# Second cross-attention: scores of all 16 heads on four row tiles of TensorE

## The chip, the cores and the metric

The kernel runs on one core of a Trainium2 chip. The metric is the device time of one execution in microseconds (us). Engines are named as in the profile: PE is TensorE's matmuls and PEld its weight loads, DVE is VectorE, ACT is ScalarE, POOL is GpSimd, SP is SyncE, which here issues the DMAs.

## The reference

The kernel computes two layers on `x` (2 batches, 128 queries, width 128) with a context of 2 x 2048 keys: cross-attention, self-attention, a mixture of experts, and then a second time cross-attention, self-attention and experts. All is float32. The change lies in the second cross-attention:

```python
rq = (iQ @ Wq.T).reshape(b, q, H, ADIM)                    # H = 16 heads of ADIM = 8
kv = (iK @ Wkv.T).reshape(b, s, 2, H, ADIM)                # iK: the context, s = 2048
rk, rv = (kv[:, :, 0], kv[:, :, 1])
scores = jnp.einsum('bqhd,bshd->bhqs', rq, rk) / sqrt(ADIM)
scores = jnp.where(mask[:, None, :, :], jnp.float32(-1e+32), scores)
t = jax.nn.relu(scores + nbias[0]); t = t * t
attn = t / (t.sum(-1, keepdims=True) + IEPS)
o = jnp.einsum('bhqs,bshd->bqhd', attn, rv).reshape(b, q, H * ADIM)
return o @ Wo.T
```

## The kernel before

Each engine has a program written out by hand in one function, and the engines meet on semaphores. An instruction that waits holds up all behind it on its engine.

**Keys and values.** During the first layer's self-attention and experts, gaps of TensorE are filled with the keys and values of the second cross-attention (`fill`, L623 and L628). The keys lie transposed: partition = key dimension (head x 8 + d), column = key. Each key block of 512 columns is copied by ScalarE as float32 and as float32r (`k1_hi`, rounded), and POOL subtracts (L1145) to get the rest, `k1_lo`. Products of float32r operands run in one pass of TensorE; a plain float32 matmul makes two records in the profile.

**The key stack.** The 16 heads are four groups `g` of four heads, 32 key dimensions each. SP then issues 16 DMAs (L441) that copy `k1_hi` and `k1_lo` within SBUF into `kstack`: for each group, the same 32 rows four times, hi, lo, hi, lo, so that one matmul on 128 rows sums hi x hi, lo x hi, hi x lo and lo x lo. The query is made to fit: `q1` is made for each group with its 32 rows repeated four times (four products of `wq1`, L739), ScalarE scales it (L1023), VectorE rounds it and puts the rest in rows 64 to 127 (`q1s`, L1373 and L1374), and `spread_q` (L357) multiplies it with the table `headsel` to give `qbd`: four copies side by side, each with one head's rows and zeros elsewhere. VectorE spreads the first of the eight blocks (batch, group), POOL the others.

**The loop.** A unit `m` is one batch, one group of four heads and two key blocks of 128: 4 heads x 2 blocks x 128 queries = 1024 columns, two PSUM banks. There are 64 units; units m, m+1, m+2 use three slots of two banks in turn. Eight units with the same batch and group follow each other. For each unit
- TensorE: `scores1(m)`, four matmuls of 256 columns (L762), after it waited for the slot's last user, unit m-3;
- VectorE: for seven units of eight one instruction (L1390) that takes the maximum with the negated bias and the minimum with `cap` (mask) and writes `w_ring` (three buffers); ScalarE squares it into `p_ring` (L1057, three buffers);
- for the first unit of eight: ScalarE relu into `w_first` (L1037), POOL multiplies by `keep` (L1156) and squares into `p_first` (L1160). In ScalarE's program this relu stands ahead of the square of the last unit of the eight before;
- TensorE: `weigh_v`, eight matmuls (L783) that weigh the values of nine columns (8 and one of ones) with the probabilities, on four column tiles of 32 columns. Its units run behind: two `scores1`, then two `weigh_v` of units four and more back. Of each eight the first unit (the one through POOL) is weighed last.

When the eight units of a batch and group are weighed, ScalarE copies 128 columns to `oT1` (eight copies). After the loop eight transposes (L800), the division by the sums, the output product and the layer norm follow; self-attention and experts close the kernel.

**Entry.** After the experts of the first layer come the layer norm (VectorE), two transposes, ScalarE's copy `xnT` (L885), the query product, and meanwhile on VectorE a memset of two PSUM banks (L1366) and the making of `keep` (L1368). SP issues the expert weights of the second layer behind the `kstack` DMAs, and some small weights after the last scores.

Of the kernel before, what the change touches and what calls it, by code (L numbers as in the profile page):

```python
# [16 lines left out]
F32 = mybir.dt.float32  # L17
# [7 lines left out]
P = 128  # L25
# [9 lines left out]
QUAD = 4  # L35
NQ = B * H // QUAD
# [57 lines left out]
def build(nc, ins, out):  # L94
    with ExitStack() as ctx:
# [3 lines left out]
        def bc(ap, axis, n):  # L99
# [77 lines left out]
        keep = A.take("keep", (P, B, 2 * S))  # L177
# [39 lines left out]
        cmp1 = A.take("cmp1", (P, 3, B, E1, E1))  # L217
        comb = A.take("comb", (P, B, E1))
# [15 lines left out]
        qbd = A.take("qbd", (P, B, 4, 4, S), F32R)  # L234
# [6 lines left out]
        A = Arena(nc, ctx_at, end)  # L241
# [3 lines left out]
        attn1 = A.take("attn1", (P, B, H, DA))  # L245
        attn1T = A.take("attn1T", (P, T))
# [6 lines left out]
        A2 = Arena(nc, attn0_at, attn0_at + B * H * DH * 4)  # L253
        q1 = A2.take("q1", (P, 4, T))
        q1s = A2.take("q1s", (P, 4, T), F32R)
# [5 lines left out]
        wq1 = A.take("wq1_sb", (P, 4, P))  # L261
# [9 lines left out]
            "w1", "w2", "ctxT2", "mask", "l1w", "kstack", "exp1", "sa")}  # L271
# [32 lines left out]
        q1s_done, qbd_pool = sem("q1s_done"), sem("qbd_pool")  # L304
# [59 lines left out]
        UNITS = NBLK // 2  # L364
        COMBOS = B * 4
        NU = COMBOS * UNITS
        WEIGH_LAG = 3
# [25 lines left out]
        def _(sp):  # L393
# [32 lines left out]
            get(wq1[:], "wq1", "l1w")  # L426
# [34 lines left out]
        def _(pe):  # L461
# [276 lines left out]
            for g in range(4):  # L738
                last = mm(ps[:, g // 2, (g % 2) * T:(g % 2 + 1) * T], wq1[:, g, :], xnT[:], start=True, stop=True)  # L739
                if g % 2:  # L740
                    last.then_inc(q1_psum, 1)
            pe.wait_ge(load["kstack"], 16 * 16)

            def scores1(m):

                c, u = m // UNITS, m % UNITS
                b, g = c // 4, c % 4
                if m >= 3:
                    if is_first(m - 3):
                        pe.wait_ge(relu_done, c_of(m - 3) + 1)  # L750
                    else:
                        pe.wait_ge(w1_done, nth(m - 3))
                if m == 0:
                    pe.wait_ge(qbd_done, 1)
                    pe.wait_ge(q1_done, 2)
                elif u == 0:
                    pe.wait_ge(qbd_pool, c)
                for i in range(2):
                    at = b * CTX + (2 * u + i) * P
                    for a in range(2):  # L760
                        dst = ps[:, 2 * (m % 3) + a, :].rearrange("p (h i s) -> p h i s", h=2, i=2)[:, :, i, :]
                        last = mm(dst, kstack[:, g, at:at + P], qbd[:, b, g, 2 * a:2 * a + 2, :],  # L762
                                  start=True, stop=True)
                last.then_inc(s1_psum, 1)

            def weigh_v(n):


                c, u = n // UNITS, (n + 1) % UNITS
                b, g = c // 4, c % 4  # L770
                if u == 1 and c >= 2:
                    pe.wait_ge(o1_copied, c - 1)
                if u == 0:
                    pe.wait_ge(sq_pool, c + 1)
                    p = p_first[:]
                else:
                    at = nth(c * UNITS + u)
                    pe.wait_ge(sq_done, at)
                    p = p_ring[:, (at - 1) % 3, :]
                for i in range(2):  # L780
                    k = 2 * u + i
                    for j in range(4):
                        last = mm(ps[HR * j:HR * j + DA + 1, 6 + c % 2, 0:S], v1[:, b * NBLK + k, 4 * g + j, :],  # L783
                                  p[:, (2 * j + i) * S:(2 * j + i + 1) * S],
                                  start=(k == 2), stop=(k == 1))
                last.then_inc(pv1_done, 1)
# [3 lines left out]
            for m in range(0, NU + WEIGH_LAG + 1, 2):  # L790
                for i in range(2):
                    if m + i < NU:
                        scores1(m + i)
# [779 lines left out]
```

## Time and profile before

| | us |
|---|---|
| median of 3 runs | 501.92 (499.99 to 502.14) |
| profiled execution | 502.57 |
| its span, first to last instruction | 500.8 |
| PE / PEld busy | 460.4 / 365.0 |
| DVE / ACT / POOL busy | 344.3 / 269.1 / 92.1 |

Busy times are unions of records; matmuls overlap in the array, so a busy PE need not be at its peak. The first cross-attention takes up to about 277 us; the loop of the second lies between 376.6 and 450.3 us.

### The profile page before, as it was taken

The page shows a single profiled execution, that of the slowest core. Times are in us where ns is not written, and L with a number is a line of the kernel's source. Part 1 is how long each engine was busy: PE and PEld are TensorE (multiplying, and loading weights), DVE is VectorE, ACT ScalarE, POOL GpSimd, SP SyncE. Part 2 cuts the span into 40 slices and gives each one's busy share as a digit, 9 for nine tenths or more (in the row PEclk, how much of TensorE's full clock was granted, in tenths as well). Part 3 has the DMA queues.
Part 4 walks back from the last instruction along what each step waited for, and adds up shares of the span by engine and source line. Part 5 has one row for each costly group of instructions (what it writes and reads, how often), then busy time and mean ns, then how long its engine had stood idle before and what let it go on. Part 6 is the DMA issues. An engine that isn't in the chain of part 4 may idle for free.

```text
span 500.8 us, 8175 instructions
## 1 busy us (share of the span) xinstructions
PE 460.4 (92%) x3294; PEld 365.0 (73%) x3294; DVE 344.3 (69%) x558; ACT 269.1 (54%) x441; POOL 92.1 (18%) x78
## 2 busy tenths in 40 slices
PE   6887999999999999999999898689978999986896
PEld 4665888888888888888888764368456788864685
DVE  3697767767767767767756446661478999974474
ACT  3345565565565565565564325440017999982244
POOL 0273000000000000000001234610005756530023
PEclk9799999999999999999999989979999999998799
DMA  7800000000000000000093300049995000010000
GB/s 263 335 2 0 0 2 1 0 1 0 1 1 2 1 0 1 0 2 0 1 389 151 112 1 1 0 84 209 209 202 236 3 3 3 2 30 0 2 0 12
DMA packets 6693, 28.34 MB, mean 57 GB/s; under 512 B 1920, under 2 KB 3712, under 8 KB 4864
## 3 DMA queue, kind: packets, MB, share of 16 engines
q1 hardware_dynamic: 6656, 27.82, 18.6%
q8 instruction: 26, 0.43, 0.4%
q14 instruction: 11, 0.09, 0.1%
HBM read 19.30 MB, written 0.13 MB: 39 GB/s over the span
## 4 chain that ended last, share of the span: by engine, by line
PE 64%; DVE 14%; SPq 6%; issue 6%; ACT 5%; DMA 5%; POOL 0%; POOLq 0%; DVEq 0%; ACTq 0%
PE ps L530 11%; PE ps L546 6%; PE ps L548 6%; PE ps L547 6%; PE ps L512 6%; SPq L441 5%; PE ps L514 5%; PE ps L513 5%; DMA kstack<-k_lo 3%; PE ps L856 3%; PE ps L762 3%; PE ps L783 3%; DVE w_ring L1390 3%; DVE max L1235 2%; DMA ctxT_raw<-in_ctx_t 1%
## 5 line engine op out<-in xcount | busy, mean ns | idle before, releaser
L885 ACT ACTIVATE pT_hi<-ps 128x512 fp32r<-128x512 f32 x128 | 77.0, 602 | 91.7 <-PE ps L530 91.7
L1230 DVE TENSOR_TENSOR pT_lo<-ps,pT_hi 128x512 fp32r<-128x512 f32 x128 | 86.5, 689 | 41.3 <-ACT pT_hi L885 40.8
L1235 DVE TENSOR_REDUCE max<-ps 128x1 f32<-128x1024 f32 x64 | 78.3, 1223 | 26.8 <-PE ps L514 25.0
L929 ACT ACTIVATE probs<-ps,nmax 128x1024 f32<-128x1024 f32 x64 | 71.6, 1119 | 19.0 <-DVE nmax L1267 19.0
L530 PE MATMUL ps<-ident_sb,probs 128*128 128x128 f32 x512 | 76.9, 273 | 1.2 <-DVE pT_lo L1230 0.8
L530 PEld LDWEIGHTS ps<-ident_sb,probs 128*128 128x128 f32 x512 | 63.4, 141 | 18.1 <-DVE pT_lo L1230 1.5
L1390 DVE SCALAR_TENSOR_TENSOR w_ring<-ps,neg_nbias,cap 128x1024 f32<-128x1024 f32 x56 | 67.6, 1277 | 3.4 <-PE ps L762 3.4
L1057 ACT ACTIVATE p_ring<-w_ring,nbias_sb 128x1024 f32<-128x1024 f32 x56 | 62.2, 1146 | 1.5 <-DVE w_ring L1390 0.8
L512 PE MATMUL ps<-ctxT_hi,qk_hi 128*128 128x512 f32 x128 | 56.7, 443 | 4.8 <-ACT probs L929 3.4
L546 PE MATMUL ps<-pT_hi,ctx_hi 128*128 128x512 f32 x128 | 56.5, 441 | 0.0
L514 PE MATMUL ps<-ctxT_lo,qk_hi 128*128 128x512 f32 x128 | 51.4, 402 | 0.0
L513 PE MATMUL ps<-ctxT_hi,qk_lo 128*128 128x512 f32 x128 | 51.0, 398 | 0.0
L548 PE MATMUL ps<-pT_hi,ctx_lo 128*128 128x512 f32 x128 | 50.5, 395 | 0.0
L547 PE MATMUL ps<-pT_lo,ctx_hi 128*128 128x512 f32 x128 | 50.0, 391 | 0.0
L1118 POOL MEMSET vx<- 128x32 f32 x1 | 0.2, 158 | 231.0 <-PE ps L530 231.0
L762 PE MATMUL ps<-qbd,kstack 128*128 128x256 f32 x256 | 39.6, 296 | 3.3 <-DMA kstack<-k_lo 2.6
L762 PEld LDWEIGHTS ps<-qbd,kstack 128*128 128x128 f32 x256 | 32.6, 190 | 10.8 <-issue 4.6
L783 PE MATMUL ps<-p_ring,v 128*9 128x128 f32 x896 | 30.9, 273 | 2.3 <-ACT p_ring L1057 2.1
L512 PEld LDWEIGHTS ps<-ctxT_hi,qk_hi 128*128 128x128 f32 x128 | 24.6, 192 | 10.7 <-ACT probs L929 2.9
L514 PEld LDWEIGHTS ps<-ctxT_lo,qk_hi 128*128 128x128 f32 x128 | 24.6, 192 | 5.8
L548 PEld LDWEIGHTS ps<-pT_hi,ctx_lo 128*128 128x128 f32 x128 | 24.0, 188 | 5.5
L513 PEld LDWEIGHTS ps<-ctxT_hi,qk_lo 128*128 128x128 f32 x128 | 24.9, 194 | 3.2
(207 smaller groups left out, 651.0 us busy)
## 6 DMA issues: line engine op xcount, KB each, us to landing
w_sb<-in_w SPq DMA_DIRECT2D x2, 2048.0 KB, 14.2
kstack<-k_hi SPq DMA_DIRECT2D x8, 512.0 KB, 10.0
kstack<-k_lo SPq DMA_DIRECT2D x8, 512.0 KB, 12.1
ctx_raw<-in_ctx_nat SPq DMA_DIRECT2D x2, 1024.0 KB, 13.0
ctxT_raw<-in_ctx_t SPq DMA_DIRECT2D x1, 2048.0 KB, 7.5
wg_sb<-in_wg SPq DMA_DIRECT2D x1, 1088.0 KB, 14.0
wu_sb<-in_wu SPq DMA_DIRECT2D x1, 1088.0 KB, 16.2
wd_sb<-in_wd SPq DMA_DIRECT2D x1, 1088.0 KB, 18.3
```

What stands on the lines that cost most here:

```text
L512: mm(ps[:, c, :], qk_hi[:, h, b, :], ctxT_hi[:, cols], start=True, stop=False)
L513: mm(ps[:, c, :], qk_lo[:, h, b, :], ctxT_hi[:, cols], start=False, stop=False)
L514: last = mm(ps[:, c, :], qk_hi[:, h, b, :], ctxT_lo[:, cols], start=False, stop=True)
L530: last = nc.tensor.transpose(ps[:, turn_bank(n), j * S:(j + 1) * S], probs[:, q % 2, j, k * P:(k + 1) * P], ident[:])
L546: mm(acc, ctx_hi[:, row, :], pT_hi[:, n % 3, :], start=(k == 0), stop=False)
L547: mm(acc, ctx_hi[:, row, :], pT_lo[:, n % 3, :], start=False, stop=False)
L548: mm(acc, ctx_lo[:, row, :], pT_hi[:, n % 3, :], start=False, stop=(k == NBLK - 1)).then_inc(pv_done, 1)
L762: last = mm(dst, kstack[:, g, at:at + P], qbd[:, b, g, 2 * a:2 * a + 2, :], start=True, stop=True)
L885: return nc.scalar.activation(dst, src, ACT.Copy)
L1230: v.tensor_tensor(pT_lo[:, n % 3, :], ps[:, turn_bank(n), :], pT_hi[:, n % 3, :], ALU.subtract).then_inc(lo_done, 1)
L1235: return v.tensor_reduce(max2[:, p:p + 1], ps[:, 2 * p:2 * p + 2, :], AX.XY, ALU.max)
L1390: v.scalar_tensor_tensor(w_ring[:, (at - 1) % 3, :].rearrange("p (h n) -> p h n", h=4), ps[:, bank:bank + 2, :].rearrange("p a (h n) -> p ...
```

## The change

The key stack and its 16 DMAs are gone. `scores1(i)` takes one key block and all 16 heads: four row tiles of 32 rows, one for each group, read their 32 partitions of `k1_hi` or `k1_lo` directly, and three matmuls accumulate in each tile's own bank: hi x hi, lo x hi, hi x lo (the product lo x lo is dropped). That is 12 matmuls of 512 columns for two units; in the order of issue the four tiles of one product come together. A unit is now one key block and eight heads (two groups), still 1024 columns and two banks, and the two units of a pair are ready after the third product. The pair waits for both slots. The query is one product (L739 once), copied twice by ScalarE (rounded `q1_hi`, and `q1`), `q1_lo` by one subtraction; `qbd` has a block for each batch and hi or lo, the first two spread by VectorE, the other two by POOL before its second round. The values of a batch accumulate in one bank for all groups; ScalarE copies 512 columns once for each batch. `keep` has one block of 128 queries for each eight units (1024 columns). The rings move to other addresses since the keys stay in use. The waits of ScalarE's relu and its place in the program are as before.

```diff
@@ SP
-            sp.wait_ge(mo_proj, 1)
-            sp.wait_ge(kv_act, 2 * NKV)
-            sp.wait_ge(k1_split, NKV)
-            for t in range(4):
-                part = k1_lo if t % 2 else k1_hi
-                for g in range(4):
-                    sp.dma_start(kstack[32 * t:32 * t + 32, g, :].bitcast(F32),
-                                 part[32 * g:32 * g + 32, :].bitcast(F32)).then_inc(load["kstack"], 16)
-            get(wq1[:], "wq1", "l1w")
+            get(wq1[:].rearrange("p (g c) -> p g c", g=4), "wq1", "l1w", ins["wq1"][:, :, 0:HR])
@@ constants and helpers
-        UNITS = NBLK // 2
-        WEIGH_LAG = 3
+        OCT = 8
+        WEIGH_LAG = 4
-        def spread_q(engine, c):
-            b, g = c // 4, c % 4
-            return engine.tensor_tensor(qbd[:, b, g, :, :], bc(q1s[:, g, b * S:(b + 1) * S], 1, 4),
+        def spread_q(engine, b, lo):
+            q = q1_lo if lo else q1_hi
+            return engine.tensor_tensor(qbd[:, b, lo, :, :], bc(q[:, b * S:(b + 1) * S], 1, 4),
                                         bc(headsel[:], 2, S), ALU.mult)
+        def weighed(n):
+            return n - n % OCT + (n + 1) % OCT
+        def score_slot(m):
+            at = 2 * (m % 3)
+            return ps[:, at:at + 2, :]
@@ TensorE
-            for g in range(4):
-                last = mm(ps[:, g // 2, (g % 2) * T:(g % 2 + 1) * T], wq1[:, g, :], xnT[:], start=True, stop=True)
-            pe.wait_ge(load["kstack"], 16 * 16)
+            mm(ps[:, 0, 0:T], wq1[:], xnT[:], start=True, stop=True).then_inc(q1_psum, 1)
+            pe.wait_ge(k1_split, NKV)
+            pe.wait_ge(q1_done, 2)
+            def scores1(i):
+                b = i // NBLK
+                for m in (2 * i - 3, 2 * i - 2):
+                    if m >= 0 and is_first(m):
+                        pe.wait_ge(relu_done, c_of(m) + 1)
+                    elif m >= 0:
+                        pe.wait_ge(w1_done, nth(m))
+                if i == NBLK:
+                    pe.wait_ge(qbd_pool, 2)
+                for t, (part, lo) in enumerate(((k1_hi, 0), (k1_lo, 0), (k1_hi, 1))):
+                    if i == 0 and t != 1:
+                        pe.wait_ge(qbd_done, 1 + lo)
+                    for g in range(4):
+                        rows = slice(HR * g, HR * g + HR)
+                        last = mm(score_slot(2 * i + g // 2)[:, g % 2, :], part[rows, i * P:(i + 1) * P],
+                                  qbd[rows, b, lo, :, :].rearrange("p j s -> p (j s)"),
+                                  start=(t == 0), stop=(t == 2))
+                        if t == 2 and g % 2:
+                            last.then_inc(s1_psum, 1)
...
+            for m in range(0, NU + WEIGH_LAG, 2):
+                if m < NU:
+                    scores1(m // 2)
+                if m >= WEIGH_LAG:
+                    weigh_v(m - WEIGH_LAG)
+                    weigh_v(m - WEIGH_LAG + 1)
@@ ScalarE
-            def copy_o1(c):
-                act.wait_ge(pv1_done, UNITS * (c + 1))
-                copy(oT1[:, c, :], ps[:, 6 + c % 2, 0:S]).then_inc(o1_copied, 1)
+            def copy_o1(b):
+                act.wait_ge(pv1_done, NU // B * (b + 1))
+                copy(oT1[:, 4 * b:4 * b + 4, :].rearrange("p g s -> p (g s)"), ps[:, 6 + b, :])\
+                    .then_inc(o1_copied, 1)
@@ VectorE
-            v.tensor_scalar(keep[:], cap[:].rearrange("p (b k) s -> p b (k s)", b=B)[:, :, 0:2 * S], neg_nbias[:],
+            v.tensor_scalar(keep[:], cap[:].rearrange("p (i k) s -> p i k s", k=OCT // 2)[:, :, 0, :], neg_nbias[:],
                             None, ALU.is_gt).then_inc(keep_done, 1)
+            dve.wait_ge(q1_done, 1)
+            spread_q(v, 0, 0).then_inc(qbd_done, 1)
+            dve.wait_ge(q1_done, 2)
+            v.tensor_tensor(q1_lo[:], q1[:], q1_hi[:], ALU.subtract).then_inc(q1_split, 1)
+            dve.wait_ge(q1_split, 1)
+            spread_q(v, 0, 1).then_inc(qbd_done, 1)
...
                 v.scalar_tensor_tensor(
-                    w_ring[:, (at - 1) % 3, :].rearrange("p (h n) -> p h n", h=4),
-                    ps[:, bank:bank + 2, :].rearrange("p a (h n) -> p (a h) n", h=2), neg_nbias[:],
-                    bc(cap[:, k:k + 2, :].rearrange("p i s -> p (i s)"), 1, 4), ALU.max, ALU.min)\
+                    w_ring[:, (at - 1) % 3, :].rearrange("p (h s) -> p h s", h=8),
+                    score_slot(m).rearrange("p a (h s) -> p (a h) s", h=4), neg_nbias[:], bc(cap[:, m // 2, :], 1, 8),
+                    ALU.max, ALU.min).then_inc(w1_done, 1)
```

## Rows read from the trace of the kernel before

**Rows 1.** Chain that ended last, loop; start us, us, what

```profile
389.58 1.15 PE ps L762 x8
390.73 0.99 PE ps L783 x32
```

**Rows 2.** Busy time by engine in one stretch of the loop

```profile
core 0: us, PE busy (x) PEld busy (x) DVE busy (x) ACT busy (x) POOL busy (x), PEclk, DMA share, GB/s
...
389.00:407.00 18.00, 17.73 (x344) 14.60 (x332) 17.35 (x16) 17.87 (x20) 11.06 (x7) 1.00 0.01 3
```

**Rows 3.** VectorE in order of time; start, duration, what, idle before

```profile
378.00 9.63 DVE L1390 SCALAR_TENSOR_TENSOR w_ring<-ps,neg_nbias,cap 128x1024 f32<-128x1024 f32 x8 [1.21 <-PE ps L762]
387.82 8.52 DVE L1390 SCALAR_TENSOR_TENSOR w_ring<-ps,neg_nbias,cap 128x1024 f32<-128x1024 f32 x7 [0.20 <-PE ps L762]
396.71 8.43 DVE L1390 SCALAR_TENSOR_TENSOR w_ring<-ps,neg_nbias,cap 128x1024 f32<-128x1024 f32 x7 [0.37 <-PE ps L762]
```

**Rows 4.** Line L1390, ns min/median/max; idle before it, times

```profile
L1390 DVE SCALAR_TENSOR_TENSOR w_ring<-ps,neg_nbias,cap x56: 1274/1276/1285, 378.0 to 446.5; 128x1024 f32<-128x1024 f32 x56
...
  PE ps L762: 3.4, 8
```

**Rows 5.** Line L1057, ns min/median/max

```profile
L1057 ACT ACTIVATE p_ring<-w_ring,nbias_sb x56: 1134/1146/1156, 379.3 to 447.8; 128x1024 f32<-128x1024 f32 x56
```

**Rows 6.** ScalarE in order of time, one round

```profile
403.86 1.10 ACT L1037 ACTIVATE w_first<-ps,nbias_sb 128x1024 f32<-128x1024 f32 x1
404.85 3.22 ACT L1057 ACTIVATE p_ring<-w_ring,nbias_sb 128x1024 f32<-128x1024 f32 x3
```

**Rows 7.** All engines in order of time, entry of the loop

```profile
371.62 0.38 ACT L885 ACTIVATE xnT<-ps 128x256 f32<-128x256 f32 x1 [20.72 <-PE ps L468]
...
372.12 0.42 DVE L1368 TENSOR_SCALAR keep<-cap,neg_nbias 128x512 f32<-128x512 f32 x1
373.22 0.60 ACT L1023 ACTIVATE q<-ps 128x512 f32<-128x512 f32 x1 [1.22 <-PE ps L739]
...
374.64 0.69 DVE L357 TENSOR_TENSOR qbd<-q1s,headsel_sb 128x512 fp32r<-128x512 f32 x1
...
376.64 1.69 PE L762 MATMUL ps<-qbd,kstack 128*128 128x256 f32 x12 [2.60 <-DMA kstack<-k_lo]
...
377.43 1.11 ACT L1037 ACTIVATE w_first<-ps,nbias_sb 128x1024 f32<-128x1024 f32 x1 [2.74 <-PE ps L762]
...
378.59 0.39 PE L762 MATMUL ps<-qbd,kstack 128*128 128x256 f32 x1 [0.25 <-ACT w_first L1037]
```

**Rows 8.** Timeline of the experts' first products, fp32, 256 columns

```profile
336.15 14.05 PE L722 MATMUL ps<-xm,w_sb 128*128 128x256 f32 x64 [0.99 <-DVE xm L1346]
```

**Rows 9.** Line L762, ns min/median/max

```profile
L762 PE MATMUL ps<-qbd,kstack x256: 276/283/388, 376.6 to 445.2; 128*128 128x256 f32 x128
```

**Rows 10.** TensorE in order of time, in the loop

```profile
404.65 1.22 PE L762 MATMUL ps<-qbd,kstack 128*128 128x256 f32 x8
```

**Rows 11.** DMA issues; KB, us to landing

```profile
wq_sb<-in_wq SPq DMA_DIRECT2D x1, 256.0 KB, 2.7
```

**Rows 12.** All engines in order of time, around 280 us

```profile
277.51 0.43 SPq L395 DMA_DIRECT2D wq_sb<-in_wq  x1
...
282.75 3.80 PE L628 MATMUL ps<-wkvo_sb,ctxT_raw 128*128 128x128 f32 x32
```

**Rows 13.** TensorE in the first cross-attention; first and last of eight

```profile
23.64 0.39 PE L513 MATMUL ps<-ctxT_hi,qk_lo 128*128 128x512 f32 x1
...
25.25 0.39 PE L514 MATMUL ps<-ctxT_lo,qk_hi 128*128 128x512 f32 x1
```

**Rows 14.** TensorE at untiled and at column-tiled matmuls

```profile
310.18 1.05 PE L628 MATMUL ps<-wkvo_sb,ctxT_raw 128*128 128x128 f32 x8
311.16 1.52 PE L680 MATMUL ps<-pm,vx 128*32 128x128 f32 x48
```

**Rows 15.** ScalarE in order of time, end of the loop

```profile
450.10 0.28 ACT L885 ACTIVATE oT<-ps 128x128 f32<-128x128 f32 x1 [1.18 <-PE ps L783]
```

**Rows 16.** VectorE in order of time, around 294 us

```profile
293.66 1.21 DVE L1297 TENSOR_TENSOR kr<-ps,rope_sb 128x1024 f32<-128x1024 f32 x1
```

More of the change, by code:

```diff
@@ L35 @@
 QUAD = 4
+NU = 2 * B * NBLK
 NQ = B * H // QUAD
@@ L245, in build @@
         attn1 = A.take("attn1", (P, B, H, DA))
+        keep = A.take("keep", (P, NU // 8, S))
         attn1T = A.take("attn1T", (P, T))
@@ L252, in build @@
         diag = A2.take("diag", (P, B, E0, S))
-        A2 = Arena(nc, attn0_at, attn0_at + B * H * DH * 4)
-        q1 = A2.take("q1", (P, 4, T))
-        q1s = A2.take("q1s", (P, 4, T), F32R)
+        A2 = Arena(nc, attn0_at + B * H * DH * 2, attn0_at + B * H * DH * 4)
+        q1 = A2.take("q1", (P, T))
+        q1_hi = A2.take("q1_hi", (P, T), F32R)
+        q1_lo = A2.take("q1_lo", (P, T), F32R)
         p_first = Arena(nc, attn0_at, stage).take("p_first", (P, 1024))
@@ L260, in build @@
         rtm = A.take("rtm", (P, 2, B))
-        wq1 = A.take("wq1_sb", (P, 4, P))
+        wq1 = A.take("wq1_sb", (P, P))
         wkvo1 = A.take("wkvo1_sb", (P, 3, D))
@@ L775, in weigh_v @@
+            def weigh_v(n):
+                m = weighed(n)
+                i, half = m // 2, m % 2
+                if is_first(m):
+                    pe.wait_ge(sq_pool, c_of(m) + 1)
                     p = p_first[:]
                 else:
[L777 to L781, printed above, removed]
-                    for j in range(4):
-                        last = mm(ps[HR * j:HR * j + DA + 1, 6 + c % 2, 0:S], v1[:, b * NBLK + k, 4 * g + j, :],
-                                  p[:, (2 * j + i) * S:(2 * j + i + 1) * S],
-                                  start=(k == 2), stop=(k == 1))
+                    pe.wait_ge(sq_done, nth(m))
+                    p = p_ring[:, (nth(m) - 1) % 3, :]
+                for gg in range(2):
+                    for j in range(4):
+                        g = 2 * half + gg
+                        last = mm(ps[HR * j:HR * j + DA + 1, 6 + i // NBLK, g * S:(g + 1) * S],
+                                  v1[:, i, 4 * g + j, :], p[:, (4 * gg + j) * S:(4 * gg + j + 1) * S],
+                                  start=(n % (NU // B) == 0 and gg == 0), stop=(i % NBLK == NBLK - 1),
+                                  skip_group_check=True)
@@ L789, in _ @@
             pe.wait_ge(zeroed, 4)
[L790 to L793, printed above, removed]
-                for i in range(2):
-                    if 0 <= m + i - WEIGH_LAG - 1 < NU:
-                        weigh_v(m + i - WEIGH_LAG - 1)
-            for c in range(COMBOS):
+            for m in range(0, NU + WEIGH_LAG, 2):
[4 more added lines that the diff above has]
+                    weigh_v(m - WEIGH_LAG + 1)
+            for c in range(B * 4):
                 if c % 4 == 0:
-                    pe.wait_ge(o1_copied, c + 4)
+                    pe.wait_ge(o1_copied, c // 4 + 1)
                 last = nc.tensor.transpose(ps[:, c // 4, (c % 4) * P:(c % 4 + 1) * P], oT1[:, c, :], ident[:])
@@ L1367, in _ @@
             dve.wait_ge(cap_done, 1)
-            v.tensor_scalar(keep[:], cap[:].rearrange("p (b k) s -> p b (k s)", b=B)[:, :, 0:2 * S], neg_nbias[:],
+            v.tensor_scalar(keep[:], cap[:].rearrange("p (i k) s -> p i k s", k=OCT // 2)[:, :, 0, :], neg_nbias[:],
                             None, ALU.is_gt).then_inc(keep_done, 1)
-            for part, ready in ((slice(0, 1), 1), (slice(1, 4), 2)):
-                dve.wait_ge(q1_done, ready)
-                link(v.tensor_copy(q1s[:, part, :], q1[:, part, :]))
-                v.tensor_tensor(q1s[64:128, part, :], q1[64:128, part, :], q1s[64:128, part, :],
-                                ALU.subtract).then_inc(q1s_done, 1)
-                dve.wait_ge(q1s_done, ready)
-                if ready == 1:
-                    spread_q(v, 0).then_inc(qbd_done, 1)
-            dve.wait_ge(load["kstack"], 256)
+            dve.wait_ge(q1_done, 1)
[4 more added lines that the diff above has]
+            spread_q(v, 0, 1).then_inc(qbd_done, 1)
             for m in range(NU):
```

90 lines of the change are left out of this document (27 added, 63 removed).

## The prediction

> **What bounds the kernel now.** I began with the chain that ended last. In the second cross-attention it runs in pairs of steps of TensorE: 0.99 us for two `weigh_v` (32 records of L783) and 1.15 us for two `scores1` (8 records of L762), 2.14 us together [rows 1]. The table by stage shows that nobody is far behind: in 18.00 us of the loop TensorE is busy 17.73, VectorE 17.35 and ScalarE 17.87, at full clock [rows 2]. So the loop has no single bound, and what counts is who waits for whom. A unit is one call of `scores1` and what follows it; eight make a round, and in each the first unit goes to ScalarE (relu, L1037) and POOL, the other seven to VectorE (L1390).
>
> VectorE's own timeline gives its pace and gaps. Seven units take 8.43 us, so one starts every (8.43 - 1.276) / 6 = 1.192 us; the record is 1.276 us, since neighbours overlap by 0.084 [rows 3, 4]. All idle time before L1390 is 3.4 us in 8 waits for L762, of which 1.21 lies before the first; seven gaps of the loop share 2.2 us [rows 3, 4]. A gap also loses the overlap, so each costs 2.2/7 + 0.084 = 0.40 us, and a round is 7 x 1.192 + 0.40 = 8.74 us (the rows start 387.82 and 396.71: 8.9, with some spread). ScalarE is at (3.22 - 1.146) / 2 = 1.04 us a square and 404.85 - 403.86 = 0.99 for the relu, 8.3 us a round: it keeps up and little more [rows 5, 6].
>
> **Entry.** Today L762 starts at 376.64, released by the transfer that landed then, though its query block was ready at 374.64 + 0.69 = 375.33; the first L1390 starts at 378.00 [rows 3, 7]. Without `kstack` the chain is that of the query product:
> - The one fp32 product makes two records where the first bank took four; such records come every 14.05 / 64 = 0.22 us [rows 8]. The first ScalarE copy moves from 373.22 to 372.78 [rows 7].
> - It writes 256 columns; a copy of that size takes 0.38 us (L885) [rows 7]: `q1_hi` is there at 373.16, `q1` some 0.35 later.
> - `keep` now makes 1024 columns, not 512. VectorE's forms there go by size (0.42 for 512), so I estimate 0.69 us at 372.12, done at 372.81: hidden by the wait for `q1_hi`. At double, 0.84, it is still hidden.
> - `spread_q` for the high part: 0.69 us, to 373.90; the subtraction of 256 columns takes 0.42 (the 512 of `keep`, an upper bound), to 374.36; `spread_q` for the low part 0.69, to 375.09 [rows 7]. The products with the high query (rounds one and two of `scores1(0)`) fit beside these, the third round starts at 375.13.
> - From there one load, one round and the tail to VectorE. A load that is waited for costs 388 - 283 = 0.105 us [rows 9]; matmuls of L762 come every (1.22 - 0.283 - 0.105) / 7 = 0.119 us [rows 10]. The tail follows from today's start: 376.64 + 0.105 + 8 x 0.119 = 377.70, and L1390 starts at 378.00, so 0.30 us [rows 3, 7]. The first L1390 comes at 375.13 + 0.11 + 0.23 + 0.30 = 375.77: **2.2 us gained**. The transfer cannot give more, since the query chain is next.
>
> The smaller `wq1` load is cut into pieces of 128 bytes, four times as many. It lands 2.7 us after its issue at 277.5 today and is first needed at 282.75 [rows 11, 12]; it would have to take twice that to cost anything. I cost it at nothing (below: nothing either, as it gates only that start).
>
> **The loop: how long four row tiles take.** No row shows a product on 32 rows. `scores1(i)` issues 12 matmuls of 512 fp32r columns for two units, in three rounds of four row tiles. Today such a matmul on the full array comes every (25.25 - 23.64) / 7 = 0.23 us [rows 13]. If the four of a round run side by side, a pair takes 3 x 0.23 = 0.69 us where L762 takes 8 x 0.119 = 0.95. One after another, it is 12 x 0.23 = 2.76 us. The nearest row is column tiling in L680: untiled 128-column matmuls come every 1.05 / 8 = 0.13 us, the 48 tiled ones every 1.52 / 48 = 0.032, four times as often, with one load each [rows 14]. So tiles run fully side by side there, loads too, and I take 0.23 a round. A case between: 128-column loads, 0.105 each, that share one path make a round 4 x 0.105 = 0.42.
>
> The Trainium skill, "TensorE: Matmul & The Clock Gate", Part 3 (Measured speedup vs the span model), gives four row tiles of 32 rows and 512 columns a speedup of 3.07, not 4. By that a round is an estimated 1.3 times as long, 0.30 us, and the loop some 7 us longer than by the row of L680. No run here shows it yet.
>
> **The loop: the new waits.** TensorE's work falls, but a pair now starts only when both its slots are free, and both its units come out of the third round together. Let T be the time when `w_ring` of the seventh unit of a round is written (w1_done of 8c+6).
> - The pair with the next round's first unit is scored by T + 0.05 (wake-up: relu ends at 378.54, L762 starts at 378.59) + 0.11 + 0.69 + 0.30 = T + 1.15 [rows 7]. VectorE is free for it after unit 8c+7, at T - 0.084 + 1.192 = T + 1.11. An ordinary pair thus costs 0.04 us of waiting.
> - ScalarE squares 8c+6 first (T + 0.05, pace 1.04), then does the relu of 8c+8 (1.095): done at T + 2.18 [rows 6].
> - The next pair, 8c+10 and 8c+11, needs that relu's slot (2i-2 = 8c+8). Before the change only unit 8c+11 needed it, and 8c+10 was scored in the meantime. Now both wait: T + 2.18 + 0.05 + 0.11 + 0.69 + 0.30 = T + 3.33. VectorE has finished its only unit in between at T + 1.11 + 1.19 = T + 2.30. It stands **1.03 us in every round, where it stood 0.40**.
> - TensorE does not add to this: behind the pair stand two `weigh_v`, 0.99 us, which end near T + 2.0 even with the changes of tiling; queued behind the wait for the relu are the third-round semaphore and the `weigh_v` of units whose squares are not late.
>
> Sum: 8 gaps x 1.03 = 8.2 against 7 x 0.40 = 2.8: +5.4. Three ordinary pairs in each of 8 rounds x 0.04: +0.9. The last copy of the outputs takes 512 columns, 0.60 like L1023, where it took 0.28 [rows 7, 15]: +0.3. With six copies less ScalarE gains time that it then waits. POOL spreads two query blocks, not seven, off the path. Loop +6.6, entry -2.2: **+4.4 us**; the terms of the stall rest on tails that I could read 0.05 us too long, so I take +4.1.
>
> The form of L1390 changes from 4 x 256 to 8 x 128. A PSUM read in eight rows with a broadcast table, L1297, takes 1.21 us [rows 16], and a two-operand form, so 1.276 stays. The lower bound, 0.06 off each of 56, would give 3.4 back.
>
> The profiled execution took 502.57 us (span 500.8). 502.57 + 4.1 = 506.7; it lay 0.65 above the median of 501.92, so the forecast is **506.0 us**.
>
> **The rivals.**
> - *Faster, TensorE was the bound.* The chain shows TensorE end to end for four pairs in eight [rows 1]; with 0.26 us less in each pair the loop runs at VectorE's pace. For that the wait behind the relu must be covered, by a shorter tail and round or by a relu that comes early. Then the 2.8 us of gaps go, +0.3 for the copy, -2.2 entry: -4.7, 497.2 us. It decides at a stall below 0.13 us. Against it: square and relu alone take 2.14 us after T [rows 6]. Chance 0.13.
> - *No difference.* Tails, wake-ups and L1390 each at the low end: the stall is 0.75 us and ordinary pairs wait for nothing. Loop +3.5, or +2 with part of the bound of L1390; net about +1: 503. Chance 0.14.
> - *The tiles run only partly side by side.* Each 0.01 us of a round costs about 3 x 32 x 0.01 = 1 us, since the pair is on the path both behind the relu and between units. At 0.42 a round: +19 over the forecast, 525; at 0.92, one after another: +66, 572. By the skill's factor of 3.07 the estimate would be 513. For it: no 32-row tile in the trace, and a row tile writes all 128 partitions of its bank, unlike a column tile. Chance 0.16, mostly its mild part.
>
> My forecast has the remaining 0.57, with a range of its own of 504.3 to 508.5. About 0.5% (2.5 us) can be told from no change. Slower by more: 0.16 + nearly all of 0.57 = 0.70; within: 0.17; faster: 0.13. The range 500 to 513 leaves out most of the faster case and the serial part of the third.
>
> **What would show it.** Right: the first L1390 near 375.8; matmuls of `scores1` in groups of four that start together, groups 0.23 us apart; seven L1390 per round at 1.2 us and a gap of about 1.0 us before the second of them, whose releaser is TensorE behind the relu; a round of 9.4 us. Wrong: groups further apart than 0.26, matmuls evenly spaced, a gap below 0.6, or a first L1390 after 376.5. A granted clock below 1.00 in the loop, which TensorE's idle time could bring, would also break the sum.

## The result, and the profile after

| | before | after |
|---|---|---|
| median of 5 runs, us | 501.78 (499.99 to 502.14) | 509.16 (508.0 to 510.07) |
| profiled execution, us | 502.57 | 508.18 |
| its span, us | 500.8 | 506.4 |

The changed kernel takes 1.0155 times as long, 95% interval 1.0127 to 1.0183: 7.4 us more in the medians, 5.6 in the two profiled executions. The forecast was 506.0, with a range of 500 to 513.

The page of the changed kernel, first lines (mean clock by slice in the row PEclk):

```profile
span 506.4 us, 8405 instructions
...
PE 453.9 (90%) x3416; PEld 348.8 (69%) x3416; DVE 344.9 (68%) x556; ACT 271.0 (54%) x435; POOL 87.1 (17%) x73
...
PEclk9799999999999999999999999799978999998799
...
PE 71%; DVE 18%; ACT 6%; issue 3%; DMA 1%; POOL 0%; SPq 0%; POOLq 0%; DVEq 0%
```

Four milestones in both traces cut the difference. "Entry" runs from the start of the layer norm ahead of the second cross-attention to the first `w_ring` (L1390 before, L1375 after), "loop" from there to the end of the last:

| stretch, us | before | after | difference | forecast |
|---|---|---|---|---|
| up to that layer norm | 367.3 | 366.0 | -1.3 | 0 |
| entry | 10.75 | 8.34 | -2.4 | -2.2 |
| loop | 69.73 | 78.66 | +8.9 | +6.3 |
| to the next layer norm | 7.19 | 7.37 | +0.2 | +0.3 |
| the rest | 45.84 | 46.02 | +0.2 | 0 |

The terms of the forecast add up to +4.4 here; it took +4.1 for the whole.

The first row lies ahead of the change: in one stretch of it, 270 to 300 us, the granted clock was 0.94 in the profile of before and 1.00 in that of after. It differs as much between profiles of programs that are the same up to there: that layer norm starts at 364.2 us in e3_two_products and at 368.0 in e7_warm_one, below. So the -1.3 is not put down to the change. It makes up most of the 1.8 us by which the profiles differ less than the medians; the rest is not separated.

All engines in order of time, entry of the loop of the changed kernel (start, duration, what; it answers to [rows 7]):

```profile
369.85 0.44 PE L466 MATMUL ps<-ident_sb,xn 128*128 128x128 f32 x2 [0.51 <-DVE xn L1190]
...
370.33 0.38 ACT L876 ACTIVATE xnT<-ps 128x256 f32<-128x256 f32 x1 [20.71 <-PE ps L466]
...
370.76 0.70 PE L736 MATMUL ps<-xnT,wq_sb 128*128 128x256 f32 x2 [0.47 <-ACT xnT L876]
370.83 0.68 DVE L1359 TENSOR_SCALAR keep<-cap,neg_nbias 128x1024 f32<-128x1024 f32 x1
371.50 0.38 ACT L1014 ACTIVATE q_hi<-ps 128x256 fp32r<-128x256 f32 x1 [0.79 <-PE ps L736]
...
372.76 0.50 PE L755 MATMUL ps<-qbd,k_hi 32*128 32x512 f32 x4 [1.29 <-DVE qbd L357]
...
373.72 0.51 PE L755 MATMUL ps<-qbd,k_hi 32*128 32x512 f32 x4 [0.23 <-DVE qbd L357]
374.27 1.11 ACT L1027 ACTIVATE w_first<-ps,nbias_sb 128x1024 f32<-128x1024 f32 x1 [2.11 <-PE ps L755]
374.31 1.28 DVE L1375 SCALAR_TENSOR_TENSOR w_ring<-ps,neg_nbias,cap 128x1024 f32<-128x1024 f32 x1 [0.64 <-PE ps L755]
...
375.43 0.80 PE L755 MATMUL ps<-qbd,k_hi 32*128 32x512 f32 x4 [1.20 <-ACT w_first L1027]
...
377.12 2.48 DVE L1375 SCALAR_TENSOR_TENSOR w_ring<-ps,neg_nbias,cap 128x1024 f32<-128x1024 f32 x2 [1.53 <-PE ps L755]
```

The reader is to see three things. No load of `kstack` stands before the first L755. Matmuls of L755 come as groups of four whose starts lie within some 0.02 us, so that the view gives them one row. And the first `w_ring` is at 374.31, while the next pair is scored only at 375.43, behind the relu (374.27 + 1.11): VectorE's second unit comes 2.8 us after its first, where eight came in one run before [rows 3].

Busy time by engine and granted clock (PEclk) ahead of and over the first units (the stretches overlap) and in the steady loop of the changed kernel; the last row answers to [rows 2]. The columns are the stretch, its length, busy time (and instructions) of PE, PEld, DVE, ACT and POOL, the clock, the share of DMA and GB/s:

```profile
369.30:374.30 5.00, 2.43 (x17) 1.02 (x16) 3.71 (x7) 1.07 (x4) 0.00 (x0) 1.00 0.78 331
374.40:384.60 10.20, 7.70 (x92) 4.43 (x96) 7.09 (x6) 6.73 (x6) 6.26 (x4) 0.50 0.01 2
...
377.00:380.00 3.00, 1.53 (x16) 0.90 (x12) 2.48 (x2) 1.52 (x2) 2.92 (x3) 0.50 0.00 0
380.00:384.00 4.00, 4.00 (x60) 2.26 (x60) 2.82 (x3) 3.08 (x3) 1.86 (x2) 0.50 0.01 4
...
389.00:407.00 18.00, 14.69 (x333) 9.94 (x324) 16.59 (x14) 16.71 (x16) 7.48 (x5) 1.00 0.02 3
```

Between 374.3 and 374.4 us the granted clock fell from 1.00 to 0.50, which is the lower level of 1.2 GHz, and it stayed there until 384.6. What TensorE did before the fall: it waited for 0.51, 0.47, 1.29 and 0.23 us, ahead of the rows of 369.85, 370.76, 372.76 and 373.72. The wait for the relu had only just begun (374.23), and that wait of 1.20 us before 375.43 and the next of 1.47 before 378.55 lie in the slow stretch. The kernel before had 1.00 from 374 to 384 us, although it waited for 2.60 us in one piece ahead of 376.64 [rows 7].

VectorE in order of time in the steady loop, which answers to [rows 3]:

```profile
388.35 8.62 DVE L1375 SCALAR_TENSOR_TENSOR w_ring<-ps,neg_nbias,cap 128x1024 f32<-128x1024 f32 x7 [0.93 <-PE ps L755]
397.90 4.91 DVE L1375 SCALAR_TENSOR_TENSOR w_ring<-ps,neg_nbias,cap 128x1024 f32<-128x1024 f32 x4 [0.93 <-PE ps L755]
```

A round is 397.90 - 388.35 = 9.55 us, with one idle stretch of 0.93. TensorE in order of time there, with [rows 10, 13] before:

```profile
392.75 0.43 PE L755 MATMUL ps<-qbd,k_hi 32*128 32x512 f32 x4
393.11 1.06 PE L774 MATMUL ps<-p_ring,v 128*9 128x128 f32 x32
394.64 0.51 PE L755 MATMUL ps<-qbd,k_hi 32*128 32x512 f32 x4 [0.47 <-DVE w_ring L1375]
394.95 0.43 PE L755 MATMUL ps<-qbd,k_lo 32*128 32x512 f32 x4
395.18 0.43 PE L755 MATMUL ps<-qbd,k_hi 32*128 32x512 f32 x4
```

And the chain of waits of the changed kernel in the same stretch, where [rows 1] showed TensorE end to end (start us, us, what):

```profile
393.23 1.28 DVE w_ring L1375
394.51 0.14 issue
394.64 0.97 PE ps L755 x12
395.62 1.04 PE ps L774 x32
...
397.70 1.15 ACT p_ring L1047
```

`w_ring` of the seventh unit ends at 394.51. The pair behind it is scored from 394.64, and ScalarE then does the relu of its first unit and the squares behind it, the last of which (397.70) the chain names. The relu itself is not on this chain: it releases the pair that lets VectorE start at 397.90, and the square ends in time for the unit after that, so the two ways are nearly level. ScalarE's own timeline has the relu:

```profile
395.64 1.12 ACT L1027 ACTIVATE w_first<-ps,nbias_sb 128x1024 f32<-128x1024 f32 x1
```

### The profile page after: what moved, and what is told of

Its sections match the earlier page's. It is cut to its first block, busy times and chain, and to the rows that moved or that the text cites. A ratio compares the mean times of both kernels' runs of the same rounds, so it can differ in the third digit from the quotient of the medians.

```text
span 506.4 us, 8405 instructions
## 1 busy us (share of the span) xinstructions
PE 453.9 (90%) x3416; PEld 348.8 (69%) x3416; DVE 344.9 (68%) x556; ACT 271.0 (54%) x435; POOL 87.1 (17%) x73
## 4 chain that ended last, share of the span: by engine, by line
PE 71%; DVE 18%; ACT 6%; issue 3%; DMA 1%; POOL 0%; SPq 0%; POOLq 0%; DVEq 0%
PE ps L528 11%; PE ps L544 6%; PE ps L546 6%; PE ps L545 6%; PE ps L510 6%; DVE w_ring L1375 6%; PE ps L512 5%; PE ps L511 5%; PE ps L755 4%; PE ps L847 3%; PE ps L720 3%; PE ps L728 3%; PE ps L774 2%; DVE max L1226 2%; ACT p_ring L1047 2%
## 5 line engine op out<-in xcount | busy, mean ns | idle before, releaser
L1375 DVE SCALAR_TENSOR_TENSOR w_ring<-ps,neg_nbias,cap 128x1024 f32<-128x1024 f32 x56 | 69.0, 1280 | 10.3 <-PE ps L755 10.3
L1047 ACT ACTIVATE p_ring<-w_ring,nbias_sb 128x1024 f32<-128x1024 f32 x56 | 63.6, 1148 | 8.0 <-DVE w_ring L1375 6.1
L755 PE MATMUL ps<-qbd,k_hi 32*128 32x512 f32 x256 | 31.6, 465 | 15.3 <-DVE w_ring L1375 10.5
L774 PE MATMUL ps<-p_ring,v 128*9 128x128 f32 x896 | 32.0, 281 | 1.5 <-ACT p_ring L1047 1.5
L1147 POOL TENSOR_TENSOR w_first<-w_first,keep 128x1024 f32<-128x1024 f32 x8 | 19.2, 2395 | 82.2 <-ACT w_first L1027 82.2
L755 PEld LDWEIGHTS ps<-qbd,k_hi 32*128 32x128 f32 x256 | 14.8, 193 | 25.2 <-DVE w_ring L1375 17.0
L774 PEld LDWEIGHTS ps<-p_ring,v 128*9 128x9 f32 x896 | 21.7, 92 | 14.9 <-issue 8.3
```

Of the source, the lines that this page charges most:

```text
L1047: nc.scalar.activation(p_ring[:, (at - 1) % 3, :], w_ring[:, (at - 1) % 3, :], ACT.Square, bias=nbias[:]).then_inc(sq_done, 1)
L1375: v.scalar_tensor_tensor(w_ring[:, (at - 1) % 3, :].rearrange("p (h s) -> p h s", h=8), score_slot(m).rearrange("p a (h s) -> p (a h) s", ...
```

## Experiments

All kernels are the changed one with the edit shown. Each ran beside the kernel before; "against before" is the ratio with its 95% interval, "against after" compares medians.

### e1_warm: is it the clock?

```diff
+ keep_warm(2, 3)                 # behind the query product
  scores1(m // 2)
+ if m == 0: keep_warm(4, 3)
+ if m == 2: pe.wait_ge(w1_done, 1); keep_warm(2, 2)
```

`keep_warm(bank, n)` issues n matmuls on zeros, as elsewhere in the kernel (L474). They fill the waits ahead of and among the first units and compute nothing.

> The changed kernel with idle matmuls of zeros in TensorE's three waits at the entry of the loop: three behind the query product, three behind the first pair of scores, two behind the second pair. Theory C (clock): in the changed kernel TensorE's granted clock fell to half between 374 and 384 us because the new entry leaves TensorE short of work; each round of a pair took 0.42 us there instead of 0.23, and the first eight units took 14.0 us instead of some 10.9. With the filling the clock stays at 1.00 from 374 to 384, the first eight units take 10.5 to 11.5 us, and the time falls by about 3 us, to 506. Rival F (filling of the pipeline): the first units are slow because nothing is buffered yet and each pair waits for the unit before it; then the first eight units still take about 14 us and the time does not change (509, or a little more).

Measured: 506.31 us, 1.0096 [1.0079, 1.0113]. Windows of this kernel, where the changed one had 0.50 twice, and VectorE in order of time:

```profile
377.00:380.00 3.00, 2.59 (x48) 1.62 (x46) 3.00 (x3) 1.95 (x2) 2.92 (x3) 1.00 0.03 5
380.00:384.00 4.00, 3.05 (x64) 1.98 (x64) 4.00 (x4) 3.77 (x5) 1.90 (x2) 1.00 0.00 0
```

```profile
374.34 1.28 DVE L1381 SCALAR_TENSOR_TENSOR w_ring<-ps,neg_nbias,cap 128x1024 f32<-128x1024 f32 x1 [0.64 <-PE ps L756]
376.69 8.63 DVE L1381 SCALAR_TENSOR_TENSOR w_ring<-ps,neg_nbias,cap 128x1024 f32<-128x1024 f32 x7 [1.07 <-PE ps L756]
386.26 8.62 DVE L1381 SCALAR_TENSOR_TENSOR w_ring<-ps,neg_nbias,cap 128x1024 f32<-128x1024 f32 x7 [0.93 <-PE ps L756]
```

From the first `w_ring` to the second round it takes 11.92 us, where the changed kernel took 14.04. The loop is 2.2 us shorter in the trace (76.51) and the median 2.85: the half clock is a real part of the loss, worth two to three us. It is not the profiled execution's alone: the mean clock was 0.960 to 0.966 in the five executions of the changed kernel and 0.973 to 0.980 in the five of this one, and an estimate, 10.2 us at half speed in 506, is 0.010. The steady round is untouched, 9.55 with 0.93 idle, so the rest is not the clock.

### e2_relu_half: is it the relu?

```diff
- activation(w_first[:].rearrange(...), score_slot(m), ACT.Relu, ...)
+ activation(w_first[:, 0:512], score_slot(m)[:, 0, :], ACT.Relu, ...)
```

This kernel leaves out half of the scores of each first unit; POOL fills `w_first` with zeros once, in lines that are not shown. This kernel and all that follow, but e7_warm_one and e10_order_free, carry all the idle matmuls of e1_warm.

> As e1_warm, and ScalarE's relu of the first unit of each eight takes only one of its two banks (512 columns instead of 1024), so half of those units' scores are left out. Theory R (the wait behind the relu makes the gap of 0.93 us idle in each round): the relu's record falls from 1.12 to about 0.6 us, relu_done comes 0.5 us earlier, the gap falls to about 0.45 us and the round from 9.55 to about 9.05; over eight rounds some 3.5 to 4 us less than e1_warm. Rival T (TensorE's own work with its two changes of tiling for each pair sets the round): the relu's length does not matter, round 9.55, time of e1_warm. Rival S (ScalarE's total work sets it): 8 x 0.5 = 4 us less too, but then ScalarE would show no idle time in e1_warm; the changed kernel shows 8.0 us idle before its squares.

Measured: 503.11, 1.0042 [1.0021, 1.0063]; 3.2 us below e1_warm. ScalarE, then VectorE, in order of time:

```profile
394.19 0.69 ACT L1035 ACTIVATE w_first<-ps,nbias_sb 128x512 f32<-128x512 f32 x1
394.77 2.18 ACT L1055 ACTIVATE p_ring<-w_ring,nbias_sb 128x1024 f32<-128x1024 f32 x2
```

```profile
386.88 8.63 DVE L1384 SCALAR_TENSOR_TENSOR w_ring<-ps,neg_nbias,cap 128x1024 f32<-128x1024 f32 x7 [0.57 <-PE ps L757]
```

The relu is 0.43 us shorter and the idle stretch 0.36: the relu was on the path, nearly in full. The round is 9.20 us and the loop 74.02, 2.5 less than in e1_warm. The stretch stops at 0.57 us: TensorE now goes from the two `weigh_v` (394.08) to the next pair (395.07) without a wait, so they are next.

### e3_two_products: what does one round of four cost?

```diff
- for t, (part, lo) in enumerate(((k1_hi, 0), (k1_lo, 0), (k1_hi, 1))):
+ for t, (part, lo) in enumerate(((k1_hi, 0), (k1_lo, 0))):
```

This kernel leaves out the product of the rounded key with the rest of the query.

> As e1_warm, but the third accumulated product (rounded key with the rest of the query) is left out: two rounds of four row tiles instead of three. Theory R: the length of the scoring is on the path twice, in the chain behind the relu (0.23 us less) and in the three ordinary pairs (their wait of 0.06 us each goes, 0.19 in a round). Round 9.55 to about 9.1, idle gap 0.93 to 0.70, seven units in 8.43 instead of 8.62 us; 3 to 3.5 us less than e1_warm. Rival T (TensorE's work is the bound): 4 pairs x 0.23 = 0.93 us less a round, 7.4 us less in all. Rival N: nothing on the path, no difference.

Measured: 502.98, 1.0032 [1.0011, 1.0053]; 3.3 us below e1_warm. VectorE in order of time:

```profile
383.85 8.43 DVE L1381 SCALAR_TENSOR_TENSOR w_ring<-ps,neg_nbias,cap 128x1024 f32<-128x1024 f32 x7 [0.71 <-PE ps L756]
393.00 7.24 DVE L1381 SCALAR_TENSOR_TENSOR w_ring<-ps,neg_nbias,cap 128x1024 f32<-128x1024 f32 x6 [0.72 <-PE ps L756]
```

The idle stretch loses 0.22 us, one group of four, and the seven units go from 8.63 to 8.43: the 0.06 us that each ordinary pair waited are gone. The round is 9.15, 0.40 shorter, 8 x 0.40 = 3.2. So matmuls of a pair are on the path at 0.23 us a group and no more.

### e4_split: is it the pair?

```diff
- def scores1(i):                        # waits for slots of both units
+ def scores1(i, halves=(0, 1)):         # waits only for the slots of its halves
...
+ if m // 2 % 4 == 1: scores1(m // 2, (0,)); scores1(m // 2, (1,))
```

The second pair of each round goes out unit by unit, so only its second unit waits for the relu. No work is left out.

> As e1_warm, but the pair behind each first unit (the second pair of eight units) is scored in two halves, two row tiles at a time, the first half waiting only for its own slot and not for the relu. No work is left out. Theory R: the first unit of that pair is scored while the relu runs; its L1390 starts some 0.2 us after TensorE finished the weighing (about T + 3.1 instead of T + 3.33), at the price of two-tile rounds: the gap falls to 0.6 to 0.75, the round from 9.55 to about 9.3, 1.5 to 2.5 us less than e1_warm. Rival: two-tile rounds take as long as four-tile rounds and TensorE, with 0.8 us more in each round, becomes the bound: no gain, or up to 3 us more.

Measured: 502.25, 1.0017 [1.0005, 1.0029]; 4.1 us below e1_warm, more than expected. VectorE in order of time:

```profile
387.54 8.62 DVE L1384 SCALAR_TENSOR_TENSOR w_ring<-ps,neg_nbias,cap 128x1024 f32<-128x1024 f32 x7 [0.58 <-PE ps L756]
396.72 3.71 DVE L1384 SCALAR_TENSOR_TENSOR w_ring<-ps,neg_nbias,cap 128x1024 f32<-128x1024 f32 x3 [0.57 <-PE ps L756]
```

The round is 9.18 us and the loop 73.99, 2.5 us less than in e1_warm; the other 1.6 of the medians is not in the loop, and the traces do not explain it. The edit takes no work away, adds waits and makes the groups smaller, yet in the loop it wins as much as halving the relu: the joint wait of both units for the relu's slot was the cause. What stays idle is 0.57, as in e2_relu_half: the `weigh_v` again, behind which TensorE starts the pair (395.72) without a wait.

### e5_order: the same with TensorE's order mended

```diff
+ steps = [(0, (0, 1), 1), (1, (0,), 0), (1, (1,), 1), (2, (0, 1), 3), (3, (0, 1), 3)]
  # (pair, halves, how many weigh_v behind it)
```

> As e4_split, and the weighing is spread otherwise over each eight units: one weigh_v behind the first pair, none between the two halves of the second pair, one behind them, then three and three (in e4_split two behind each pair). No work is left out. Theory R, in the form that e2_relu_half and e4_split left it (both stopped at a gap of 0.57 us: by then not the relu but the two weigh_v that TensorE does first keep the second pair back): with only one weigh_v in front, the first half is scored 0.5 us earlier and the second while VectorE works on it. The gap falls below 0.2 us, the round from 9.2 to 8.7 to 8.9 us, the time by 2.5 to 4 us against e4_split, to 498.5 to 500, below the kernel before. Rival: the gap of 0.57 us is the length of the half rounds themselves, or squares that wait for p_ring buffers, since weighing is put off; then the round stays at 9.2 or grows and the time is 502 or more.

Measured: 501.54, 1.0005 [0.9985, 1.0025], level with the kernel before. The spacing before the second unit fell to 1.41 to 1.44 us, start to start (1.19 is VectorE's pace), and the round to about 8.8: with fewer `weigh_v` ahead of the pair the 0.57 us goes. Busy time by engine of this kernel:

```profile
389.00:407.00 18.00, 17.77 (x374) 11.79 (x374) 17.72 (x16) 17.46 (x17) 8.70 (x5) 1.00 0.02 4
```

This is the picture of [rows 2]: nobody has room. It stayed above the expected 498.5 to 500.

### e6_all_halves: what is a pair worth?

```diff
+ if m // 2 % 4 in (0, 1, 2, 3): scores1(m // 2, (0,)); scores1(m // 2, (1,))
```

No unit is scored beside another by one call any more. If two halves ran one after the other, a pair would cost six rounds.

> As e1_warm, but every pair is scored in two halves of two row tiles, each half waiting only for its own slot, which is the order of waits of the kernel before on the changed kernel's tiles. It tells what four tiles side by side are worth. If two tiles take as long as four (0.23 us a round of products), each pair costs TensorE 0.69 us more plus what it waits; TensorE does 2 x 0.7 + 1.1 + changes of tiling = 2.7 to 2.9 us for a pair, more than VectorE's 2.1 to 2.4, and becomes the bound: rounds of 10.3 us or more, 510 us or more. Rival: matmuls on two tiles run faster or the finer waits are worth more than the width: 506 us or less.

Measured: 502.76, 1.0039 [1.0018, 1.0059]. The expectation of 510 or more was wrong; the rival's 506 or less holds. TensorE in order of time, one pair in two halves, then its busy time:

```profile
402.39 0.80 PE L756 MATMUL ps<-qbd,k_hi 32*128 32x512 f32 x4
402.73 0.39 PE L756 MATMUL ps<-qbd,k_lo 32*128 32x512 f32 x2
...
403.26 0.40 PE L756 MATMUL ps<-qbd,k_hi 32*128 32x512 f32 x2
```

```profile
390.00:440.00 50.00, 49.52 (x982) 34.55 (x984) 46.63 (x40) 49.24 (x47) 22.79 (x11) 1.00 0.01 3
```

The row at 402.39 holds four records: two of the first half start there, two of the second half at 402.70, ahead of the first half's second product (402.73) and its third (402.96): halves on different row tiles interleave, although issued one behind the other. The last group starts 0.87 us after the first, where that of a full pair does so after 0.54 (394.64 to 395.18). So the split costs a third of a microsecond a pair, not 0.69. TensorE (49.52 of 50) and ScalarE (49.24) are both nearly full here; the chain that ended last runs for 88% through TensorE from 392 to 410 us.

### e7_warm_one: does one filling do?

```diff
- if m == 0: keep_warm(4, 3)
- if m == 2: pe.wait_ge(w1_done, 1); keep_warm(2, 2)     # of e1_warm; keep_warm(2, 3) stays
```

> As e1_warm, with only the first of the three fillings: three matmuls of zeros behind the query product, none behind the first and second pair of scores. Theory C: the clock falls after a stretch in which TensorE does too little; the other two waits (1.2 us behind the first pair, 1.5 behind the second) come right after this one. If the first filling is enough, the clock stays at 1.00 and the time is that of e1_warm, 506.3; if the clock needs the others, it falls some us later than in the changed kernel and part of the 3 us is lost again: 507 to 509. I expect the first (0.6).

Measured: 505.55, 1.0092 [1.0058, 1.0126]. Its six runs fall in two groups, three within 504.64 to 504.68 and three from 506.4 to 507.4; the profiled one belongs to the second. TensorE, then its windows:

```profile
379.91 0.80 PE L756 MATMUL ps<-qbd,k_hi 32*128 32x512 f32 x4 [1.46 <-DVE w_ring L1376]
```

```profile
377.00:380.00 3.00, 1.06 (x16) 0.62 (x16) 2.15 (x3) 1.77 (x3) 2.37 (x1) 0.97 0.00 0
380.00:384.00 4.00, 4.00 (x56) 2.35 (x56) 3.36 (x3) 3.18 (x3) 3.89 (x3) 0.59 0.02 4
```

The clock fell here too, at 379.85 us, behind waits of 1.20 (before 377.47) and 1.46, and it was back at 383.3: 3.5 us after the first `w_ring` where the changed kernel had it at once, and for 3.4 us where that had 10.2. So the first filled wait moves the fall and shortens it, but does not prevent it, which the expectation had as the likelier case. The loop takes 77.28 us, against 76.51 in e1_warm and 78.67 in the changed kernel. The median is level with e1_warm. Whether the clock held in the three faster executions is not shown, since none of them was profiled.

### e8_best and e9_uniform: halves everywhere, in a regular order

```diff
+ # e8: steps = [(0,(0,1),0),(1,(0,),2),(1,(1,),0),(2,(0,),2),(2,(1,),0),(3,(0,),2),(3,(1,),2)]
+ # e9: every pair in halves, two weigh_v between them, weigh_v two units later
```

> Both findings together, no work left out: the first pair of each eight units is scored four tiles wide, the other three in two halves, and two weigh_v stand between the halves of each of these pairs and two more behind the last. In e6_all_halves the two halves of a pair overlapped on TensorE (the second starts some 0.3 us after the first, on other row tiles), so a pair cost 0.3 us more and not 0.7, and its seven instructions of VectorE ran without waits (8.44 us); in e5_order the gap fell to 0.22 us. Theory R: with both, the round comes to 8.5 us (0.1 to 0.2 above the 8.34 of VectorE's own pace), the loop to some 71 us; the kernel before needed 8.74 and 72.3. With the shorter entry the time is 496.5 to 498.5, about 0.7% below the kernel before. Rival P: TensorE has become the bound (busy 49.5 of 50 us in e6_all_halves); the two more changes of tiling per pair eat the gain, round 8.8 to 9.0, time 500 to 502, no difference from the kernel before.

> As e8_best in a uniform form: every pair in two halves, two weigh_v between them, none behind; the weighing lags six units instead of four. Theory R: round 8.5 to 8.6, time within 1 us of e8_best. Rival P: one more half pair per round makes it 0.2 to 0.3 us a round longer than e8_best (2 us in all).

Measured: e8_best 501.86, 1.0001 [0.9985, 1.0017]; e9_uniform 503.22, 1.0041 [1.0021, 1.0061]. My version to beat both failed. Busy time of e8_best:

```profile
390.00:440.00 50.00, 49.85 (x978) 32.87 (x974) 47.31 (x39) 47.84 (x47) 23.05 (x11) 1.00 0.01 3
```

TensorE is busy 49.85 of 50 us, in e9_uniform all 50. With `weigh_v` between two halves they do not interleave, and each half pays its own three groups: in the trace of e8_best a half takes 0.89 us up to the next `weigh_v` (398.36 to 399.25), a full pair 0.91 (403.13 to 404.04). Every change between row tiles and column tiles costs too (0.13 us in the changed kernel, last section). The round was 9.0 us in both.

### e10_order_free: e5_order with fewer idle matmuls

```diff
- if i == 0 and halves[-1]: keep_warm(4, 3)
- keep_warm(2, 2)
+ keep_warm(2, 1)
```

> As e5_order, without the three idle matmuls behind the first pair and with one instead of two behind the second pair. In e5_order they stood before the first half of the second pair, which waits for nothing there, and VectorE's second L1390 came 2.35 us after its first. Theory R: that half now fills TensorE's wait itself; the second L1390 comes 1.2 to 1.6 us after the first, the loop falls from 71.3 to some 70.4 us, the time by 0.8 to 1 us against e5_order, to 500.6: with the entry that is 2.4 us shorter, 0.5 to 1 us below the kernel before, which may not be told from no difference. Rival C: the clock falls again as in e7_warm_one, rounds of 0.42 us for some pairs, and the time is 502 or more.

Measured: 499.46 against 501.58 for the kernel before beside it, 0.9953 [0.9937, 0.9969]: faster than both, by half a percent against the kernel before. VectorE in order of time and busy time:

```profile
373.73 47.62 DVE L1386 SCALAR_TENSOR_TENSOR w_ring<-ps,neg_nbias,cap 128x1024 f32<-128x1024 f32 x38 [0.64 <-PE ps L756]
421.50 22.48 DVE L1386 SCALAR_TENSOR_TENSOR w_ring<-ps,neg_nbias,cap 128x1024 f32<-128x1024 f32 x18 [0.15 <-ACT p_ring L1058]
```

```profile
374.00:384.00 10.00, 8.49 (x136) 5.03 (x134) 9.86 (x9) 8.92 (x9) 6.55 (x5) 1.00 0.01 2
...
390.00:440.00 50.00, 49.16 (x990) 32.07 (x992) 49.01 (x40) 48.73 (x48) 23.92 (x11) 1.00 0.01 3
```

VectorE runs 38 units in one row, with a start every (47.62 - 1.28) / 37 = 1.25 us, and TensorE keeps its full clock. The loop takes 70.25 us from the first `w_ring` to the end of the last, 0.5 more than before the change; the entry is 8.34 us as in the changed kernel, 2.4 less than before. The two make 1.9 of the 2.1 us gained.

## Why the prediction was right, and where it was short

The sign, the place and the price of the stall were right. The size was short: +4.1 was forecast and +7.4 measured, and 509.16 lies above the 504.3 to 508.5 that the forecast gave itself. What kept it within 500 to 513 is width that was meant for tiles that run partly side by side, and these did not occur: that part is luck.

- **Entry, -2.2 us: right, -2.4.** From `xnT` on each step fell as summed: `keep` 0.68 (estimate 0.69), query copies 0.38 each, `spread_q` 0.69, the first L755 beside them at 372.76. From the third group to the first `w_ring` it took 0.59 us. The `wq1` load in pieces of 128 bytes landed 2.7 us after its issue, as before, and cost nothing.
- **A round of four tiles is 0.23 us: right.** Groups start at 394.95 and 395.18, and e3_two_products moved the gap by 0.22. The first to second of a pair is 0.31, the load's wait in it. The Trainium skill, "TensorE: Matmul & The Clock Gate", Part 3 (Measured speedup vs the span model), gives a speedup of 3.07, an estimated 0.30 us a round: this trace doesn't agree; at full clock four tiles take the time of one matmul on the full array [rows 13].
- **The stall behind the relu: right in place, cause and size.** With T = 394.51: relu done at 396.76 = T + 2.25 (forecast T + 2.18), next unit at 397.90 = T + 3.39 (T + 3.33). The idle time is 0.93; the forecast's 1.03 counts the lost overlap of 0.084 too, so 0.95 in this view. e2_relu_half and e4_split take away one link each, and the idle time falls to 0.57 and 0.58, where TensorE's `weigh_v` are next; e5_order moves these too.
- **Ordinary pairs wait 0.04 us: 0.06.** (8.62 - 8.43) / 3, gone in e3_two_products.
- **L1375 costs what L1390 cost: right.** 1.28 us a record; neither bound was touched.
- **Tail, +0.3: +0.2.** The last copy took 0.60 us, where it took 0.28 [rows 15]. ScalarE of the changed kernel in order of time:

```profile
455.34 0.60 ACT L876 ACTIVATE oT<-ps 128x512 f32<-128x512 f32 x1 [1.18 <-PE ps L774]
```

- **Full clock throughout: this failed.** The sum took all rounds at 2.4 GHz. It named the clock as what would break it but put no price on it. In the new entry TensorE goes from one wait to the next (0.51, 0.47, 1.29 and 0.23 us) with little to do between them, and at 374.35 us the clock halved for 10.2 us, just as the first units began. e1_warm gives its price: 2.2 us in the trace, of the 2.6 that the loop's term was short there, and 2.85 in the median. The rest of the loop, 6.8 us, is the forecast's 6.3.
- The rival that TensorE's relief makes the kernel faster asked for a covered wait behind the relu. e5_order and e10_order_free cover most of it, and still the loop (71.29 and 70.25 us) doesn't go below the 69.73 of before: TensorE, VectorE and ScalarE are all within 3% of full. Its -4.7 us wasn't reached; e10_order_free got -2.1.

Open is how the 7.4 us of the medians divide in the executions that were not profiled. Open too is a part of the distance between e5_order and e10_order_free, 2.1 us in the medians; the edits between them are four idle matmuls. Their traces have the same entry (8.34 us) and loops of 71.29 and 70.25, so 1.0 us is the idle matmuls', as expected. Another 1.8 us lies ahead of the entry, where the two programs are the same (the layer norm starts at 367.20 and 365.39), and what makes it is not known.

## What to carry to other kernels

When work is merged into a larger step, every wait of its parts becomes a wait of the whole: look which part waits for the slowest releaser, and price the stall at that point before counting what the merged work saves. The merged form can be kept if that one step is split again (here one pair in four). And where a change leaves TensorE with one wait behind another while nothing else is queued for it, as at the entry and the first units of this pipeline, put a price for the lower clock into the sum.

## What the runs showed of the hardware

- Half matmul groups on different row tiles of 32 rows interleave with each other, though issued in sequence (the second half's first product starts at 402.70, the first half's third at 402.96): +0.33 us for a pair in halves, where one after the other would be +0.69 (e6_all_halves).
- The granted clock fell to 0.50 behind several short waits of TensorE, none over 1.5 us (0.51, 0.47, 1.29 and 0.23 us in the 5 us before 374.35, changed kernel); in e7_warm_one, with matmuls on zeros ahead of the first pair, it fell at 379.85, behind waits of 1.20 and 1.46. With all three places filled it stayed at 1.00 (e1_warm). A single wait of 2.60 us left it at 1.00 in the kernel before [rows 7].
- From the last group of four on row tiles to the first `weigh_v` on column tiles it is 0.36 us (392.75 to 393.11), 0.13 more than to a next group.
